# A fused LoRA, attention and feed-forward kernel: its prologue is reordered, its loads spread over three queues, and a projection of head 1 moved ahead of V

## The reference, cut to what matters

```python
# x (8,128,512) f32; two lists of 8 adapter ids
h = x @ W.T + b + 2 * (x @ lora_As[id_a]) @ lora_Bs[id_a]      # per sequence, rank 16
q = h @ ((qw_q - 8) * scales_q)      # 32 heads of 128; one scale per 128 input rows and column
k, v = the same with qw_k, qw_v      # 8 heads each
q, k = rope(q), rope(k)
ctx = softmax(causal(q @ k.T / sqrt(128))) @ v      # per sequence of 128
x = x + ctx @ ((qw_o - 8) * scales_o)
y = (x @ B[id_b].T) @ A[id_b].T      # rank 16, per sequence
x = x + int8_linear(gelu(int8_linear(layernorm(y), w1, b1)), w3, b3)
```

## Time and profile before

| | us |
|---|---|
| median of three runs (lowest, highest) | 636.5 (636.47, 638.72) |
| the profiled execution's own time | 636.2 |
| span of its trace | 634.4 |
| TensorE busy | 580.6 (92%) |
| VectorE busy | 514.2 (81%) |
| ScalarE busy | 331.4 (52%) |
| GpSimd busy | 412.2 (65%) |

### The profile page before, as it was taken

The page is one execution under the profiler, slowest core; times in us unless marked ns, Lnnn a source line. Parts: engine busy times, 40 slices in busy tenths (PEclk is TensorE's granted clock), DMA queues, the critical chain, the costliest instruction groups (busy, mean ns, idle before and its releaser), DMA issues. The chain is left out here.

```text
span 634.4 us, 10392 instructions
## 1 busy us (share of the span) xinstructions
PE 580.6 (92%) x3072; PEld 435.4 (69%) x3075; DVE 514.2 (81%) x670; ACT 331.4 (52%) x877; POOL 412.2 (65%) x411
## 2 busy tenths in 40 slices
PE   4979979999999999999999999999999999876664
PEld 3535557887888788878878878887888877624221
DVE  2845457998899799889988998999899888757894
ACT  2024247556555655565556556556556555305873
POOL 0000477799679779976997698689779877103663
PEclk9989999999999999999999999999999999996675
DMA  9342263412451243134113422442322111000012
GB/s 306 83 116 29 79 167 117 118 50 52 129 137 51 56 142 99 50 116 116 50 51 116 116 51 69 139 115 56 95 70 83 50 50 34 1 0 1 2 50 83
DMA packets 38551, 52.17 MB, mean 82 GB/s; under 512 B 12064, under 2 KB 20448, under 8 KB 38528
## 3 DMA queue, kind: packets, MB, share of 16 engines
q1 hardware_dynamic: 36080, 47.36, 28.3%
q10 hardware_dynamic: 2448, 4.53, 2.1%
HBM read 28.81 MB, written 2.10 MB: 49 GB/s over the span
## 5 line engine op out<-in xcount | busy, mean ns | idle before, releaser
L918 DVE SCALAR_TENSOR_TENSOR accT<-pair,so_now,accT 128x1024 f32<-128x1024 f32 x125 | 157.5, 1277 | 21.3 <-PE pair L1151 20.6
L904 DVE SCALAR_TENSOR_TENSOR raw_q<-pair,sc_now,raw_q 128x1024 f32<-128x1024 f32 x90 | 115.4, 1283 | 3.5
L1150 PE MATMUL pair<-ctx_hi,wo 128*128 128x512 f32 x256 | 104.9, 410 | 2.6 <-issue 1.5
L623 ACT ACTIVATE probs<-flow,negmax 128x128 f32<-128x128 f32 x248 | 87.3, 369 | 34.3 <-DVE negmax L869 34.3
L1150 PE MATMUL pair<-h_hi,wq 128*128 128x512 f32 x240 | 100.8, 420 | 2.8 <-ACT wq L598 1.8
L1151 PE MATMUL pair<-ctx_lo,wo 128*128 128x512 f32 x256 | 100.3, 392 | 0.0
L1151 PE MATMUL pair<-h_lo,wq 128*128 128x512 f32 x240 | 94.4, 393 | 0.0
L485 POOL TENSOR_TENSOR probs<-probs,rowinv 128x512 f32<-128x512 f32 x64 | 66.7, 1042 | 27.3 <-DVE rowinv L891 27.3
L466 POOL TENSOR_TENSOR qT<-rope_c,rope_s 128x512 f32<-128x512 f32 x62 | 79.4, 1281 | 4.4
L454 POOL TENSOR_TENSOR rope_s<-swap_q,consts 128x512 f32<-128x512 f32 x62 | 80.2, 1294 | 2.3 <-DMA swap_q<-raw_q 2.3
L454 POOL TENSOR_TENSOR rope_c<-raw_q,consts 128x512 f32<-128x512 f32 x62 | 78.5, 1287 | 1.9 <-DVE raw_q L864 1.3
(11 more groups left out here) (212 smaller groups left out, 1031.1 us busy)
## 6 DMA issues: line engine op xcount, KB each, us to landing
swap_q<-raw_q SPq DMA_DIRECT2D x62, 256.0 KB, 3.6
wq_i<-in_L_attn_qw_q SPq DMA_DIRECT2D x8, 1024.0 KB, 5.9
wo_i<-in_L_attn_qw_o SPq DMA_DIRECT2D x32, 256.0 KB, 2.7
swap_k<-raw_k SPq DMA_DIRECT2D x14, 256.0 KB, 3.6
wkv_i<-in_L_attn_qw_k SPq DMA_DIRECT2D x8, 256.0 KB, 3.9
wkv_i<-in_L_attn_qw_v SPq DMA_DIRECT2D x8, 256.0 KB, 4.2
out<-probsT SPq DMA_DIRECT2D x8, 256.0 KB, 2.0
stage<-in_x ACTq DMA_DIRECT2D x4, 256.0 KB, 6.3
```

The costliest lines, as they stand in the source:

```text
L623: e = act.activation(probs[:, 0, f, seq(b)], bank[:, seq(b)], ACT.Exp, bias=negmax[:, f, b:b + 1], accum_out=rowsum[:, f, b:b + 1])
L904: dve.scalar_tensor_tensor(out=into, in0=flat(pair[pair_of(h, (kind, j), last)][:, :, :]), scalar=sc_now[:, scale_slot(kind, h), j:j + 1], ...
L918: dve.scalar_tensor_tensor(out=a, in0=flat(pair[pair_of(h, (O, c), last)][:, :, :]), scalar=so_now[:, (h if c == 0 else h - 1) % 2, c:c + ...
L1150: pe.matmul(into[:, f, :], w, upper[:, half[f]], start=True, stop=False)
```

## The change

1. **Ids.** SP loads both lists of ids into a small SBUF tile first, waits for them, and reads each id from that tile.
2. **W, scales and bias** are issued by GpSimd instead of SP.
3. **x and W are turned tile by tile,** x0, W0, x1, W1 and so on, each with a semaphore of its own. ScalarE and VectorE copy in the same order. The identity (64 KB of the constants) is loaded first; the rest of the constants comes behind x tile 3, with its own semaphore `d_tables`, and VectorE prepares `lora_mask` and `tri_b` after the first copies.
4. **Q of head 1 becomes unit 4 and V unit 5.** Half 1 of head 0's Q (unit 3) now lives in the second half of `raw_v`; unit 4 fills `raw_q`. The waits of SP, GpSimd and TensorE change their counts from 18 to 15 (swap and cosine of head 1) and from 16 to 18 (turn of V).
5. **`dequant_q(0, 2)`** (head 2's weights) moves from head 0 of the loop to behind unit 3.

```diff
-        V_PAIRS = [pair[0], pair[1], pair[2], pair[0]]
-        Q_PAIRS = [pair[1], pair[2], pair[0], pair[1]]
+        Q_PAIRS = [pair[0], pair[1], pair[2], pair[0]]
+        V_PAIRS = [pair[1], pair[2], pair[0], pair[1]]
+        def early_home(kind, f):
+            return raw_v[:, 1, :] if kind == Q and f else raw(kind)[:, f, :]
...
         @block.sync
-            for c in range(C):
-                sp.dma_start(W_nat[c], W[seq(c), :]).then_inc(d_w[c], 16)
...
-            sp.dma_start(bias_col[:, :], bias.rearrange("(c p) -> p c", p=P)).then_inc(d_bias, 16)
+            for m, chosen in enumerate((ids_a, ids_b)):
+                sp.dma_start(ids[0:1, m, :], chosen.unsqueeze(0)).then_inc(d_ids, 16)
+            sp.wait_ge(d_ids, 32)
             for b in range(B):
-                ia = sp.value_load(ids_a[b:b + 1].unsqueeze(0), min_val=0, max_val=lora_a.shape[0] - 1)
+                ia = sp.value_load(ids[0:1, 0, b:b + 1], min_val=0, max_val=lora_a.shape[0] - 1)
...
             sp.wait_ge(early_sin, 4)
-            sp.wait_ge(early_added, 18)
+            sp.wait_ge(early_added, 15)
             swap(swap_q, raw_q, swapped_q)
...
         @block.gpsimd
+            for c in range(C):
+                pool.dma_start(W_nat[c], W[seq(c), :]).then_inc(d_w[c], 16)
...
+            pool.dma_start(bias_col[:, :], bias.rearrange("(c p) -> p c", p=P)).then_inc(d_bias, 16)
...
         @block.scalar
-            act.dma_start(consts[:, :], const_dram).then_inc(d_const, 16)
+            act.dma_start(consts[:, 0:P], const_dram[:, 0:P]).then_inc(d_const, 16)
             load_x(0)
+            act.dma_start(consts[:, P:K_END], const_dram[:, P:K_END]).then_inc(d_tables, 16)
             load_x(1)
...
             early(Q, 3, 1)
+            act.wait_ge(early_proj, 16)
+            dequant_q(0, 2)
...
-            early_wide(V, 4, pair[0])
+            act.wait_ge(early_cos, 2)
+            act.wait_ge(early_swap_q, 32)
+            early_wide(Q, 4, Q_PAIRS[0], n=1)
             act.wait_ge(early_cos, 4)
             act.wait_ge(early_swap_q, 64)
-            early_wide(Q, 5, pair[1], n=1)
+            early_wide(V, 5, V_PAIRS[0])
...
         @block.tensor
-            for b in range(HB):
-                turn_x(b, banks[b])
             for o in range(C):
+                turn_x(o, banks[o])
                 pe.wait_ge(d_w[o], 16)
...
-            pe.wait_ge(early_added, 16)
+            pe.wait_ge(early_added, 18)
             for f in range(2):
                 turn_values(f, banks[4 + f])
```

More of the change, by code:

```diff
@@ L140, in build @@
         y_q = w_q[:, :, :].rearrange("p (m s) n -> p m s n", m=2)
+        ids = sb("ids", [1, 2, B], I32)
         stats = sb("stats", [P, B, 6])
@@ L156, in build @@
         d_w = [sem(f"d_w{n}") for n in range(C)]
-        d_x = [sem(f"d_x{n}") for n in range(4)]
+        d_x = [sem(f"d_x{b}") for b in range(B)]
+        d_tables = sem("d_tables")
+        d_ids = sem("d_ids")
         d_sc, d_rows = sem("d_sc"), sem("d_rows")
@@ L348, in _ @@
             for b in range(B):
-                ib = sp.value_load(ids_b[b:b + 1].unsqueeze(0), min_val=0, max_val=low_a.shape[0] - 1)
+                ib = sp.value_load(ids[0:1, 1, b:b + 1], min_val=0, max_val=low_a.shape[0] - 1)
                 sp.dma_start(nA[:, :, b * R:(b + 1) * R],
@@ L363, in swap_half @@
                 for a, b in ((0, P // 2), (P // 2, 0)):
-                    sp.dma_start(into[a:a + P // 2, f, :], raw(kind)[b:b + P // 2, f, :]).then_inc(done, 16)
+                    sp.dma_start(into[a:a + P // 2, f, :], early_home(kind, f)[b:b + P // 2, :]).then_inc(done, 16)
             def swap(into, source, done):
@@ L412, in _ @@
         def _(pool):
+            for c in range(C):
+                pool.dma_start(W_nat[c], W[seq(c), :]).then_inc(d_w[c], 16)
+            pool.dma_start(sc_nat[:, 0:P], sc_q.rearrange("g (h n) -> (g h) n", n=P)).then_inc(d_sc, 16)
+            for j, s in enumerate((sc_k, sc_v)):
+                pool.dma_start(sc_nat[0:C * NKV, (1 + j) * P:(2 + j) * P],
+                             s.rearrange("g (h n) -> (g h) n", n=P)).then_inc(d_sc, 16)
+            pool.dma_start(so_nat, sc_o).then_inc(d_sc, 16)
+            pool.dma_start(bias_col[:, :], bias.rearrange("(c p) -> p c", p=P)).then_inc(d_bias, 16)
             def copy_scale(slot, column, made):
@@ L422, in early_part @@
             def early_part(table, source, into, f, done):
-                pool.tensor_tensor(per_seq(into[:, f, :]), per_seq(source[:, f, :]), on_each_seq(table), ALU.mult).then_inc(done, 1)
+                pool.tensor_tensor(per_seq(into[:, f, :]), per_seq(source), on_each_seq(table), ALU.mult).then_inc(done, 1)
             def early_add(count, f, target, parts, done):
@@ L456, in q_cosine @@
                     def q_cosine(f):
-                        ready = (early_added, 18) if first and h == 0 else (dve_drained, drains_by(g, h - 1, (Q, 3), first, last))
+                        ready = (early_added, 15) if first and h == 0 else (dve_drained, drains_by(g, h - 1, (Q, 3), first, last))
                         q_part(cos, raw_q, rope_c, ready, q_cos, f)
@@ L611, in early @@
                 act.wait_ge(early_proj, 4 * u + 1)
-                act.activation(raw(kind)[:, f, :], banks[0], ACT.Copy,
+                act.activation(early_home(kind, f), banks[0], ACT.Copy,
                                scale=sc_now[:, scale_slot(kind, n), 0:1]).then_inc(early_first, 1)
@@ L683, in body @@
                     dequant(wo[:, h % 2, :], wo_i[:, h % 2, :], wo_made)
-                    if present(h, (Q, 0), first, last):
+                    if present(h, (Q, 0), first, last) and not (first and h == 0):
                         dequant_q(g + (h + 2) // REP, (h + 2) % REP)
@@ L827, in keep_rest @@
                                          in1=h_hi[:, c, half[f]], op0=ALU.add, op1=ALU.subtract).then_inc(lo_made, 1)
+            dve.wait_ge(d_tables, 16)
+            dve.tensor_scalar(lora_mask[:, :], low_mask, 2.0, None, ALU.mult).then_inc(mask_made, 1)
+            dve.tensor_copy(tri_b[:, :], consts[:, K_TRI:K_TRI + P]).then_inc(consts_made, 1)
+            dve.wait_ge(mask_made, 1)
             quantise_weights(0)
@@ L845, in early_groups @@
             def early_groups(kind, u, f, n=0):
-                into = raw(kind)[:, f, :]
+                into = early_home(kind, f)
                 dve.wait_ge(early_first, u + 1)
```

50 lines of the change are left out of this document (20 added, 30 removed).

## The result

The changed kernel takes **626.54 us** (median of four runs, 625.89 to 629.09), the kernel before 636.49 beside it (635.93 to 638.72). The ratio is 0.9835, with a 95% interval of 0.9811 to 0.9859: 9.95 us faster. In a later session five runs gave 626.49 against 637.73, a ratio of 0.983 (0.981 to 0.985). The forecast was 627.1, in a range of 624.0 to 632.0. The profiled execution of after was the slowest of its four, 629.09, with a span of 627.3; a second one, of the later session, took 627.18, with a span of 625.3.

What follows compares the result with a forecast made beforehand. TensorE, busy 92% of the span, was taken as the bound, with gains only in its idle or low-clock stretches. Terms -2.1 - 4.65 - 1.75 - 0.88 = -9.4 took 636.2 to 626.8, plus 0.3: 627.1 us, range 624.0 to 632.0.

Steps and rivals of the forecast that it cites:

- the sign of being wrong: Way into the loop: the forecast is wrong if the first loop product is early by less than 8 us.
- The stall, -4.65: TensorE's wait ahead of the LoRA rows for the last adapter: gone with ids read from SBUF, -4.65 us.
- a uniform 2.1 us: SP's adapter loop: about 2.1 us for each adapter instead of 3.0, with an SBUF id read at 0.47.
- The clock, -1.75: First group of LoRA rows: without idle time before it the clock stays up, 5.24 us becomes 3.49, -1.75.
- The start, -2.1: Prologue up to linear(0): turning x and W starts it at 13.0 instead of 15.11, -2.1 us.
- The floor of -3.4: Start: ScalarE's first copy at 9.3, four copies at 0.6 us end at 11.7, so at most -3.4.
- The entrance, -0.88: Way into the loop: ScalarE's drain of Q follows the exponentials directly at 93.45 instead of 94.33, -0.88 us.
- TensorE is the busy engine there, so I see no such wait: Loop: no wait there gives the gain back; the argument against the rival given 1%.
- The rival that had 1%: Loop: the gain does not reach the end, being given back at a wait there; chance 1%.
- VectorE's cover: Last turn of rounded weights: VectorE's eighth tile ready between 39 and 41, TensorE at 41.2; cost nothing, at worst 1 us.
- The rival of GpSimd's lateness: Start: W comes too late from GpSimd, gaining nothing or losing up to 1.8 us; 629.2 to 631.0, chance 18%.
- the second cover: SP's K and Q loads start near 23 rather than 34.8, their users shifted by 8 us only: no cost.

Runs made afterwards that it cites:

- part 1 alone: Kernel before with only the ids loaded into SBUF and read there, W, scales and bias still on SP: 631.24 us against 637.55, ratio 0.99.
- the gap was filled instead: Kernel before with eight extra unread products on TensorE in the gap ahead of the LoRA rows: 637.11 us, ratio 0.9995.
- Part 2 without it: Changed kernel with ids read from HBM again in the loop, all else as changed: 630.41 us, and 629.26 in a second session.
- filled gap, five products: Kernel before with five extra unread products on TensorE ahead of the wait for the adapters: 636.01 us, ratio 0.9985.

## Why the prediction was right, and where it wasn't

- **The result** is 0.6 us from the forecast, on the side of *faster*, as given. The first product of the loop comes at 82.97 for 92.38, 9.4 us earlier, where less than 8 would have been the sign of being wrong. One such sign did show in part: in after TensorE waits 0.94 us for a tile of W.
- **The stall, -4.65.** Measured -4.81, and 6.3 us with the clock when part 1 was made alone. The last adapter left at 22.96 where the prediction put the loop's end at 22.5, but the way there was another. The loop started at 2.7 and not at 5.7, since a load of 32 bytes doesn't take what a tile of x does; the read cost 0.27 and not 0.47; and in place of a uniform 2.1 us the intervals run from 1.7 to 3.8, because the issues of the B loads swell. The two errors cancelled, so that the instant fits is luck.
- **The clock, -1.75.** Right: -1.75 in the instants of after and -1.69 where the gap was filled instead. The claim that nothing else was needed held in the trace.
- **The start, -2.1.** The term least known, and the one with the widest bounds. The profiled execution shows -1.24, the second -2.83, and the variants up to -3.7. The prediction had the transposes fast from 10.9 us on; in the traces of kernels that turn tile by tile that comes anywhere from 6.1 to 13, and `linear(0)` moves by 2.5 us between executions, for this reason and the arrivals. The floor of -3.4, which is 11.7, was undercut: 11.37 with W on SP, where ScalarE's copies begin at 9.08, much as forecast, but follow each other by 0.48 us and not by 0.6.
- **The entrance, -0.88.** Measured -0.86 in the instants of after, by the very mechanism: SP's swap at 79.04, which is 36.66 after the start of `linear(4)` for 39.70 before, three microseconds sooner as the prediction had it, and the drain directly behind the exponentials. That holds for six of ten profiles; in four the late swap of K left nothing of it, a wait that the prediction doesn't have. And **"TensorE is the busy engine there, so I see no such wait" is the step that failed.** The loop gave the gain back in steps of 0.1, which hang on one load more in ScalarE's list: from `linear(4)` to the first product of the tail it is 510.20 us before, 510.26 in the first profile of after and 509.92 in the second. The rival that had 1% was in part true.
- **VectorE's cover** held, and narrowly: its eighth tile was rounded at 41.3 (40.89 + 0.43), later than the 39 to 41 of the prediction, and TensorE's turn of it started at 41.94. In the other profiles of kernels that turn tile by tile and have ids in SBUF it has 0.3 to 0.6 us to spare. VectorE waited 2.71 us for the first feed-forward tile, which landed late in the fuller burst, as the prediction had it.
- **The rival of GpSimd's lateness** fell as far as the time goes: 0.5 to 0.6 us an issue, and W in SBUF 4.8 us (tiles 0 and 1) and 6.9 us (2 and 3) after it. The Trainium skill, DMA: Bandwidth & Descriptors (Issuing engine by pattern), calls SP's path generally faster for plain loads. By medians, 626.03 on SP for 626.49 to 626.54 on GpSimd, no run here can tell the two apart; the landings of W's first two tiles, 3.9 us after issue from SP there and 4.8 from GpSimd in after, agree with it, but in the kernel with part 1 alone it is 5.3 from SP. Nor was there any starving of GpSimd's loads, which the Trainium skill, SBUF — State Buffer (the box on DVE blocking DMA), allows for: they were issued by 6.4 us and VectorE began its rounding at 16.65, so this kernel doesn't test that rule.
- **Which part did it.** The prediction gave the stall to part 1. Part 2 without it closes it too, with almost nothing to spare. And the prediction named the second cover only as loads that now come early; that SP's second round of ids held the first swap back by 4.1 us already, and that part 1 is what keeps this out of the way of a TensorE 8 us earlier, it didn't see. Of the gain of 10 to 11 us part 1 brings 6.3 by itself. The rest is mostly the start, where undoing the tile-by-tile turning alone costs 5 us; the start wasn't tried by itself on the kernel before. The entrance brings at most 0.9, and little that lasts.

## What to carry to other kernels

Look at what a queue does between its loads: eight small reads of ids from HBM and the plain loads ahead of them held back everything that TensorE did later, and a wait of 4.65 us cost 6.3 with the low clock behind it. Close such a gap with some slack, and look at what the same queue has to do behind it: a transfer that is just in time in one execution may be late in the next. And where two sets of tiles come from different queues, take them in turn, in the order in which they land.

## What the runs showed of the hardware

- The issue of a 32 KB load on SP takes 0.45 us in most cases and up to 2.56 us in after (from 11.20, while 282 to 339 GB/s moved). In the kernel before, with 3 us between adapters, it took 0.44 and 0.45 at 381 and 272 GB/s, so the other queues' loads alone don't do it; what does is open.
- A register read of an id costs 0.27 us from SBUF, against 0.84 and 0.47 (pointer and value) from HBM, up to 3.98 in the burst.
- At the start the granted clock reads 1.00 while four fp32 transposes of 128x128 follow each other by 0.86 to 1.1 us, and later by 0.5; the change comes anywhere from 6 to 16 us, and in the kernel with four tiles of x first `linear(0)` is still slow at 14.78. There the durations tell the state, and the granted clock doesn't.
- Waits of 1.77 and 1.82 us were followed by a granted clock of 0.50 at the way into the loop (filled gap, five products); after waits of 1.77 and 1.00 at the same place in before it stayed at 1.00.
- One DMA issue more in ScalarE's list ahead of a loop made one wait in each looped group of heads 0.09 us longer (0.28 for 0.19), and taking it out again put it right.
